# A spectral mixing stage whose blocks run over column wave numbers, with VectorE turning the combined spectrum

## The chip, the cores and the metric

The kernel runs on one NeuronCore of a Trainium2 chip. The metric is the time of one execution on the device, in microseconds (us), lower is better. All data are float32. TensorE (PE) multiplies and transposes into PSUM (8 banks of 512 float32 in each of 128 partitions), VectorE (DVE) and ScalarE (ACT) move PSUM to SBUF, GpSimd (POOL) works on SBUF alone, and SyncE (SP) issues most DMAs.

## The reference, cut to what matters

The program is two blocks of a network on an image of 8 samples, 32 channels, 64 x 64 points: a spectral convolution, a mixture of experts on the tokens, four sweeps of a convolution, and a second mixture of experts. Only the first part, the spectral convolution, is touched:

```
def _L0_conv_ref(x, w1_real, w1_imag, w2_real, w2_imag):     # x: (8, 32, 64, 64), layer-normed over channels
    xf = jnp.fft.rfft2(x, norm='forward')
    w1 = jax.lax.complex(w1_real, w1_imag)                   # each (32 in, 32 out, 32, 32)
    w2 = jax.lax.complex(w2_real, w2_imag)
    top = jnp.einsum('bixy,ioxy->boxy', xf[:, :, :32, :32], w1)
    bot = jnp.einsum('bixy,ioxy->boxy', xf[:, :, -32:, :32], w2)
    out_fft = jnp.zeros((8, 32, 64, 33), dtype=xf.dtype)
    out_fft = out_fft.at[:, :, :32, :32].set(top)
    out_fft = out_fft.at[:, :, -32:, :32].set(bot)
    return jnp.fft.irfft2(out_fft, s=(64, 64), norm='forward')
...
x = x + _L0_conv_ref(_ln_c(x), ...)
```

So each of 64 x 32 kept wave numbers has a complex 32 x 32 matrix of its own, which is applied to 8 samples.

## The kernel before, in words

Everything is written by hand as one instruction list per engine; semaphores are the only order between the lists, and each engine runs its own list strictly in order. The large SBUF regions RA, RB, RCD (halves RC and RD) and RE are reused from step to step. The touched stretch has these steps; "c" is one of 8 chunks of 4 column wave numbers (ky), "g" one of 8 groups of 1024 elements a partition.

- **Turning rows (L511 to L518, `turn_halves` L435).** After the width DFT, TensorE transposes 8 groups of the half spectrum from RC; ScalarE and VectorE drain four each into RA (`t1_pairs`, L802 and L970).
- **Spectrum (L523).** `spectrum(c)`: 8 matmuls with the height DFT table for chunk c into banks 0 to 3 (two chunks in flight). The partitions of the result are 4 samples x 32 channels. `spectrum(0)` waits for all drains, with 20 filler matmuls ahead (`keep_warm`, L483); 30 more stand ahead of the first mix.
- **Spread (`xb_pairs`, L818 on ACT, L990 on DVE).** Each engine copies its half of a chunk into XB (in RB), a matrix that is block diagonal over four groups q of row wave numbers. That takes 16 copies of 32 partitions x 256 elements a chunk, 8 on each engine; consecutive elements are written 512 elements apart.
- **Mix (L539).** 64 matmuls a chunk, against the 2 MB of weights of that chunk, which SP loads from HBM into one of three buffers (L363); the products leave banks 4 to 7 by two ACT copies (L827) and two DVE copies (L999).
- **Turning the products (L560 to L571).** Per chunk TensorE transposes the products with the imaginary and with the real part (16 transposes each); ACT copies the first to `imtmp` (L832); DVE subtracts and adds (L1010, L1011) into V (RA).
- **Turning the spectrum, height DFT back.** TensorE transposes V a second time (`turn_spectrum`, 16 transposes a chunk, ACT drains, L837), and `dft_h(g)` (L584, 8 matmuls a group, two PSUM slots) follows, drained by DVE (`if2_pairs`, L1016).
- **Width DFT back.** `turn_image(g)` (16 transposes, ACT drain L837), `dft_w_back(g)` (L614, 8 matmuls 128 x 128 x 128 with a block-diagonal table), DVE adds the input (L1023) from RC, into which SP reloads the 4 MB of `x_in` (L366) once all products are turned.

ACT's list in the turning stage, which a later step refers to:

```
for c in range(NCH):
    act.wait_ge(s_t1, c + 1)
    if c >= 2:
        act.wait_ge(s_comb, c - 1)
    act.copy(imtmp[:, c % 2, :], banks(4 * (c % 2) + 2, 2)).then_inc(s_tmp, 1)
```

The functions:

Of the kernel before, what the change touches and what calls it, by code (L numbers as in the profile page):

```python
# [9 lines left out]
P = 128  # L10
BL, BH = P // C, B * C // P
TOK = H * W
KY = W // 2
# [28 lines left out]
def build_kernel(nc, x_in, dft, wspec, conv_w, conv_b, gate_w, gate_b, w1, w2, b2, own, out):  # L42
# [5 lines left out]
    with ExitStack() as ctx:  # L48
# [51 lines left out]
        s_tf, s_td = sem("turned_full"), sem("turned_drained")  # L100
# [34 lines left out]
        XB = RB[:, :].rearrange("p (s x z r q b) -> p s x z r q b", s=2, x=X8, z=2 * KYC, r=2, q=Q)  # L135
# [3 lines left out]
        V = RA[:, :].rearrange("p (c x a r n) -> p c x a r n", c=NCH, x=X8, a=2, r=2)  # L139
        V_of_b = RA[:, :].rearrange("p (c m b) -> p c m b", c=NCH, b=B)  # L140
        WR = RE[:, :].rearrange("p (s a x y n) -> p s a x y n", s=3, a=2, x=X8, y=KYC)
        imtmp = RE[:, 0:2 * 1024].rearrange("p (s n) -> p s n", s=2)
# [41 lines left out]

        def turn_slot(g):

            return banks(2 * (g % 2), 2)
# [9 lines left out]
        def t1_pairs(j):  # L197
            g = j - G_T1
            return [(RA[:, 1024 * g:1024 * g + 1024].rearrange("p (n a m) -> p a n m", n=8, a=2),
                     slot(j).rearrange("p (a n m) -> p a n m", n=8, a=2))]  # L200

        def xb_pairs(c, first):
            pairs = []
            for bl in (first, first + 1):
                for q in range(Q):
                    i = PS[C * bl:C * bl + C, 2 * (c % 2):2 * (c % 2) + 2, :].rearrange(
                        "p h (z q r x) -> p q h z r x", q=Q, r=2, x=X8)
                    o = XB[C * q:C * q + C, c % 2, :, :, :, q].rearrange("p x z r (h b) -> p b h z r x", h=BH)
                    pairs.append((o[:, bl], i[:, q]))
            return pairs  # L210
# [4 lines left out]
        def t2_pairs(c):  # L215
            pairs = []
            for bh in range(BH):
                o = RB[:, :].rearrange("p (t k b o) -> p t b k o", t=BH, k=KY, b=BL)[:, bh, :, KYC * c:KYC * c + KYC]
                i = turn_slot(c).rearrange("p (a t b y o) -> p t a b y o", a=2, t=BH, b=BL, y=KYC // 2)[:, bh]
                pairs.append((o.rearrange("p b (a y) o -> p a b y o", a=2), i))  # L220
            return pairs

        def if2_pairs(g):
            o = RD.rearrange("p (t h r k) -> p t r h k", t=BH, h=H, r=2)[:, g % 2, :, :, 8 * (g // 2):8 * (g // 2) + 8]
            return [(o, dft_slot(g).rearrange("p (k r h) -> p r h k", k=8, r=2))]
# [204 lines left out]
        def _(pe):  # L430
# [15 lines left out]

            def centre_group(ln, g):
# [55 lines left out]
            for g in range(8):  # L503
                if g == 3:
                    pe.wait_ge(s_gpc, 1)
                if g >= 4:
                    wait_one_drained(pe, G_T1 + g - 4)
                for n in range(8):
                    m = turn_halves(2 * (g % 4), n, blk(RC, 8 * g + n))
                m.then_inc(s_full, 1)  # L510


            def spectrum(c):
                if c == 0:
                    wait_one_drained(pe, G_T1 + 4)
                    keep_warm(0, 20)
                    wait_drained(pe, G_T1 + 7)
# [3 lines left out]
                for bh in range(BH):  # L521
                    for y in range(KYC):
                        m = pe.matmul(blk(PS[:, 2 * (c % 2) + bh, :], y), blk(RA, bh * KY + c * KYC + y), fwd_h,  # L523
                                      start=True, stop=True)
# [3 lines left out]
            def mix(c):  # L528
                pe.wait_ge(s_xbd, c + 1)
                pe.wait_ge(s_xba, c + 1)  # L530
                pe.wait_ge(s_wc[c % 3], 16 * (c // 3 + 1))
                for k in range(4):
# [12 lines left out]
            for c in range(NCH):  # L545
                if c + 1 < NCH:
                    spectrum(c + 1)
# [674 lines left out]
```

## Time and profile before

| what | value |
|---|---|
| median of 3 runs | 591.72 us (589.74 to 591.88) |
| profiled execution | 587.68 us, its span 585.9 us |
| busy share of the span | PE 90%, DVE 59%, ACT 51%, POOL 20% |
| mean granted TensorE clock | 0.962 |

The profile lists for each engine when an instruction ran, how long the engine was idle before it, and what ended that idle time. A float32 matmul stands there as two passes, so 8 matmuls show as x16; a transpose is one pass. Times inside the span are counted from its start. The touched steps lie between about 42 and 163 us.

### The profile page before, as it was taken

The page shows a single profiled execution, that of the slowest core. Times are in us where ns is not written, and L with a number is a line of the kernel's source. Part 1 is how long each engine was busy: PE and PEld are TensorE (multiplying, and loading weights), DVE is VectorE, ACT ScalarE, POOL GpSimd, SP SyncE. Part 2 cuts the span into 40 slices and gives each one's busy share as a digit, 9 for nine tenths or more (in the row PEclk, how much of TensorE's full clock was granted, in tenths as well). Part 3 has the DMA queues.
Part 4 walks back from the last instruction along what each step waited for, and adds up shares of the span by engine and source line. Part 5 has one row for each costly group of instructions (what it writes and reads, how often), then busy time and mean ns, then how long its engine had stood idle before and what let it go on. Part 6 is the DMA issues. An engine that isn't in the chain of part 4 may idle for free.

```text
span 585.9 us, 25109 instructions
## 1 busy us (share of the span) xinstructions
PE 528.1 (90%) x11076; PEld 472.0 (81%) x11076; DVE 344.6 (59%) x815; ACT 300.3 (51%) x838; POOL 114.7 (20%) x240
## 2 busy tenths in 40 slices
PE   8978997999965999978999999979999999767997
PEld 8978987899964985767888999969998888656873
DVE  2758997734437936773545455435555455569726
ACT  4557997643377502454444444424445777667100
POOL 4000000000034000001333333553331033461000
PEclk9999998999998899998999999979999999978979
DMA  8940882070000000000000023430000244500007
GB/s 347 369 144 2 303 326 96 3 287 1 2 4 2 2 22 0 1 1 2 4 5 3 4 51 74 109 65 6 3 3 4 40 75 80 101 9 1 2 2 288
DMA packets 50260, 41.69 MB, mean 71 GB/s; under 512 B 44998, under 2 KB 45126, under 8 KB 48934
## 3 DMA queue, kind: packets, MB, share of 16 engines
q1 hardware_dynamic: 49304, 38.51, 20.5%
q8 instruction: 89, 1.46, 1.1%
q0 software_dynamic: 704, 1.18, 0.9%
q10 hardware_dynamic: 144, 0.39, 0.2%
q14 instruction: 19, 0.16, 0.1%
HBM read 27.49 MB, written 4.19 MB: 54 GB/s over the span
## 4 chain that ended last, share of the span: by engine, by line
PE 70%; DVE 16%; ACT 5%; POOL 4%; issue 3%; SPq 1%; DMA 0%; POOLq 0%; ACTq 0%; DVEq 0%
PE PS L755 38%; PE PS L724 5%; DVE RB L990 5%; PE PS L483 4%; PE PS L614 3%; PE PS L674 3%; PE PS L584 3%; PE PS L435 2%; PE PS L462 2%; PE PS L539 2%; POOL RE L393 2%; POOL RCD L396 2%; PE PS L492 2%; DVE sums L1032 1%; PE PS L684 1%
## 5 line engine op out<-in xcount | busy, mean ns | idle before, releaser
L755 PE MATMUL PS<-RE,conv_sb 128*64 128x64 f32 x6048 | 231.2, 230 | 4.3 <-DVE RE L1131 3.9
L755 PEld LDWEIGHTS PS<-RE,conv_sb 128*64 128x64 f32 x6048 | 209.1, 139 | 26.4 <-DVE RE L1131 4.6
L880 ACT COPY PS<-convb_sb 128x64 f32<-128x64 f32 x504 | 108.2, 215 | 112.8 <-DVE RE L1143 89.7
L1143 DVE SCALAR_TENSOR_TENSOR RE<-PS,RCD 128x64 f32<-128x64 f32 x252 | 56.7, 225 | 58.0 <-PE PS L755 50.4
L405 POOL COPY RCD<-RE 128x128 f32<-128x128 f32 x126 | 37.4, 297 | 154.3 <-DVE RE L1143 154.2
L1143 DVE SCALAR_TENSOR_TENSOR RE<-PS,RE 128x64 f32<-128x64 f32 x126 | 32.6, 259 | 28.3 <-PE PS L755 26.9
L1143 DVE SCALAR_TENSOR_TENSOR RE<-PS,RB 128x64 f32<-128x64 f32 x126 | 28.4, 225 | 28.1 <-PE PS L755 20.2
L818 ACT COPY RB<-PS 32x256 f32<-32x256 f32 x64 | 40.5, 633 | 7.5 <-PE PS L523 6.7
L990 DVE COPY RB<-PS 32x256 f32<-32x256 f32 x64 | 40.3, 630 | 5.7 <-PE PS L523 4.9
L539 PE MATMUL PS<-RE,RB 128*64 128x64 f32 x1024 | 33.3, 227 | 5.1 <-DVE RCD L999 2.5
L483 PE MATMUL PS<-warm 128*128 128x128 bf16 x468 | 34.3, 239 | 3.9 <-DVE warm L908 1.4
L539 PEld LDWEIGHTS PS<-RE,RB 128*64 128x64 f32 x1024 | 32.2, 142 | 6.5 <-DVE RB L990 3.7
L393 POOL TENSOR_TENSOR RE<-RA 128x1024 f32<-128x1024 f32 x3 | 5.7, 1895 | 160.6 <-ACT RA L851 160.6
L483 PEld LDWEIGHTS PS<-warm 128*128 128x128 bf16 x468 | 31.3, 108 | 4.9 <-ACT RB L858 1.6
L913 DVE TENSOR_REDUCE sums<-RE 128x32 f32<-128x1024 f32 x16 | 19.4, 1218 | 23.2 <-ACT RE L790 23.2
L1032 DVE TENSOR_REDUCE sums<-RE 128x32 f32<-128x1024 f32 x16 | 19.2, 1202 | 19.5 <-POOL RE L393 15.8
L724 PE MATMUL PS<-RCD,espread 128*128 128x512 f32 x64 | 30.5, 632 | 0.0
L837 ACT COPY RB<-PS 128x512 f32<-128x512 f32 (+1 forms) x24 | 16.2, 735 | 25.9 <-PE PS L435 25.9
L790 ACT ACTIVATE RE<-PS 128x1024 f32<-128x1024 f32 x16 | 16.3, 1022 | 23.2 <-PE PS L462 20.1
L405 POOL COPY RB<-RE 128x128 f32<-128x128 f32 x63 | 18.7, 296 | 40.7 <-DVE RE L1143 40.7
L779 ACT COPY RCD<-PS 128x256 f32<-128x256 f32 (+1 forms) x40 | 17.6, 510 | 15.2 <-PE PS L492 7.7
L724 PEld LDWEIGHTS PS<-RCD,espread 128*128 128x128 f32 x64 | 12.8, 206 | 14.9 <-issue 14.4
(116 smaller groups left out, 715.0 us busy)
## 6 DMA issues: line engine op xcount, KB each, us to landing
RE<-wspec SPq DMA_DIRECT2D x8, 2048.0 KB, 8.5
RA<-x_in SPq DMA_DIRECT2D x8, 512.0 KB, 7.4
RCD<-x_in SPq DMA_DIRECT2D x1, 4096.0 KB, 13.7
out<-RA SPq DMA_DIRECT2D x8, 512.0 KB, 2.9
RCD<-RB SPq DMA_DIRECT2D x58, 64.0 KB, 2.6
RE<-RCD SPq DMA_DIRECT2D x32, 80.0 KB, 2.6
conv_sb<-conv_w SPq DMA_DIRECT2D x1, 768.0 KB, 20.0
w_sb<-w SPq DMA_DIRECT2D x2, 264.0 KB
```

Source lines behind the costliest of these rows:

```text
L405: pool.tensor_copy(o, i).then_inc(s_arc, 1)
L483: pe.matmul(PS[:, bank, 0:P], warm[:, :], warm[:, :], start=True, stop=True)
L539: m = pe.matmul(o[:, x % 2, y], XB[:, c % 2, x, 2 * y + a].rearrange("p r q b -> p (r q b)"), WR[:, c % 3, a, x, y, :], start=True, stop=True)
L724: pe.matmul(PS[:, 4 + k % 4, :], espread[:, BL * bh:BL * bh + BL, :].rearrange("p b o -> p (b o)"), rhs, start=True, stop=True).then_inc(s ...
L755: m = pe.matmul(conv_bank(s, u, c)[o:o + OC], conv_sb[:, s, d, o:o + OC], prev, start=False, stop=(d == 2), skip_group_check=True)
L779: m = act.copy(o, i)
L818: m = act.copy(o, i)
L880: act.copy(banks_of, convb_sb[:, s:s + 1].unsqueeze(2).to_broadcast([P, c1 - c0, n])).then_inc(s_seed, 1)
L913: dve.tensor_reduce(sums[:, 32 * g:32 * g + 32], square[:, g % 2, 0:1024].rearrange("p (a c) -> p a c", c=C), AX_X, ALU.add).then_inc(s_su ...
L990: m = dve.tensor_copy(o, i)
L1032: dve.tensor_reduce(sums[:, 32 * g:32 * g + 32], square[:, g % 2, 0:1024].rearrange("p (a c) -> p a c", c=C), AX_X, ALU.add).then_inc(s_su ...
L1143: dve.scalar_tensor_tensor(out=state[:, state_slot(s, u), b0:b1, 1:1 + HO], in0=conv_bank(s, u, c), scalar=0.0, in1=row_at(SRC[s], s, q, u ...
```

## The change

Four things change, all in the stretch above; the rest of the program is as it was, one or more lines lower in the file.

1. The mixing blocks q run over the 4 column wave numbers of a chunk. The rows are turned and drained so that the spectrum of a chunk leaves TensorE with (ky, channel) on its partitions; a chunk is then spread by 4 copies of 32 partitions x 1024 elements in place of 16 of 256. The first two spectra stand between the row groups, and the 50 filler matmuls are gone. The weights are laid out on the host to match.
2. VectorE writes the combined spectrum in another order and turns it itself in 32 x 32 blocks (`dve.transpose`); TensorE's second turn and its ACT drains are gone.
3. The height DFT back, `dft_h(c - 3)`, stands after the products of chunk c in TensorE's list. It has one PSUM slot (banks 6 and 7; group 6 uses banks 0 and 1), and ACT drains it, after `imtmp` of chunk c.
4. The width DFT back is done in four quadrants of 64 x 64, with the nonzero blocks of the table only.

```diff
-        XB = RB[:, :].rearrange("p (s x z r q b) -> p s x z r q b", s=2, x=X8, z=2 * KYC, r=2, q=Q)
+        XB = RB[:, :].rearrange("p (s x r q b) -> p s x r q b", s=2, x=H, r=2, q=KYC)
-        V = RA[:, :].rearrange("p (c x a r n) -> p c x a r n", c=NCH, x=X8, a=2, r=2)
-        V_of_b = RA[:, :].rearrange("p (c m b) -> p c m b", c=NCH, b=B)
+        V = RA[:, :].rearrange("p (c n r x a) -> p c n r x a", c=NCH, n=KYC * B, r=2, x=X8)
+        VT = RB[:, :].rearrange("p (t k n) -> p k t n", t=BH, k=KY)
+        YH = RE[:, WCOLS:WCOLS + NF]
...
+        def product_view(b0):
+            return banks(b0, 2).rearrange("p (a x r n) -> p r n x a", a=2, x=X8, r=2)
+        def dft_h_slot(g):
+            return banks(0 if g == 6 else 6, 2)
...
-        def xb_pairs(c, first):
...
+        def xb_pair(c, q):
+            rows = slice(C * q, C * q + C)
+            i = banks(2 * (c % 2), 2)[rows].rearrange("p (b x r) -> p x r b", b=B, r=2)
+            return XB[rows, c % 2, :, :, q], i
...
         @block.tensor
...
+            def quad(bank, n, lhs, table):
+                for a in range(2):
+                    rows = slice(MO * a, MO * (a + 1))
+                    for o in range(2):
+                        cols = slice(MO * o, MO * (o + 1))
+                        m = pe.matmul(PS[cols, bank + a, MO * n:MO * (n + 1)], lhs[rows, cols], table[rows, rows],
+                                      start=True, stop=True)
+                return m
...
-            spectrum(0)
+            for j in range(8):
+                turn_rows_of(j)
+                if j == 3:
+                    spectrum(0)
+                if j == 5:
+                    spectrum(1)
             for c in range(NCH):
-                if c + 1 < NCH:
+                if 1 <= c < NCH - 1:
                     spectrum(c + 1)
-                if c == 0:
-                    keep_warm(7, 30)
                 mix(c)
...
+            def dft_h(g):
+                pe.wait_ge(s_vt, 2 * (g // 2) + 2)
+                if g == 6:
+                    pe.wait_ge(s_tmp, NCH)
+                elif g >= 1:
+                    pe.wait_ge(s_dr, min(g, 6))
+                for n in range(8):
+                    m = pe.matmul(blk(dft_h_slot(g), n), blk(RB, KY * (g % 2) + 8 * (g // 2) + n), inv_h,
+                                  start=True, stop=True)
+                m.then_inc(s_df, 1)
+            for c in range(NCH):
+                turn_products(c)
+                if c >= 3:
+                    dft_h(c - 3)
+            for g in range(NCH - 3, NCH):
+                dft_h(g)
...
                 for n in range(8):
-                    m = pe.matmul(blk(dft_slot(g), n), blk(RB, 8 * g + n), inv_w, start=True, stop=True)
+                    m = quad(4 + 2 * (g % 2), n, blk(RB, 8 * g + n), inv_w)
...
         @block.scalar
...
-                act.copy(imtmp[:, c % 2, :], banks(4 * (c % 2) + 2, 2)).then_inc(s_tmp, 1)
...
+                act.copy(imtmp[:, c % 2], product_view(0)).then_inc(s_tmp, 1)
+                if c >= 4:
+                    drain_dft_h(c - 4)
+            for g in range(NCH - 4, NCH):
+                drain_dft_h(g)
...
         @block.vector
...
+                by_re, by_im = product_view(2 + 2 * (c % 2)), imtmp[:, c % 2]
+                dve.tensor_tensor(V[:, c, :, 0], by_re[:, 0], by_im[:, 1], ALU.subtract)
+                dve.tensor_tensor(V[:, c, :, 1], by_re[:, 1], by_im[:, 0], ALU.add).then_inc(s_comb, 1)
+                dve.wait_ge(s_comb, c + 1)
+                dve.transpose(VT[:, KYC * c:KYC * c + KYC],
+                              RA[:, 1024 * c:1024 * c + 1024].rearrange("p (k t n) -> p k t n", k=KYC, t=BH)
+                              ).then_inc(s_vt, 1)
```

In the changed `turn_products(c)` TensorE waits for `imtmp` of chunk c - 1 (`s_tmp`), since the imaginary products have one slot (banks 0 and 1), and for the combination of chunk c - 2 (`s_comb`) before the real ones.

**TensorE, from the last mix to the width DFT, before** (L435 transposes, L584 height DFT, L614 width DFT; each row a run of like instructions):

```order
L539 MATMUL PS<-RE,RB 64x2x32 x128
L435 MATMUL PS<-dft_sb,RCD 128x64 x256
L435 MATMUL PS<-dft_sb,RA 128x64 x64
L584 MATMUL PS<-dft_sb,RB 128x128 x16
L435 MATMUL PS<-dft_sb,RA 128x64 x32
L584 MATMUL PS<-dft_sb,RB 128x128 x16
L435 MATMUL PS<-dft_sb,RA 128x64 x32
L584 MATMUL PS<-dft_sb,RB 128x128 x32
L435 MATMUL PS<-dft_sb,RCD 128x64 x32
L614 MATMUL PS<-dft_sb,RB 128x128 x8
```

and now (L436 transposes, L591 height DFT, L454 quadrants of the width DFT):

```order
L550 MATMUL PS<-RE,RB 64x2x32 x128
L436 MATMUL PS<-dft_sb,RCD 128x64 x128
L591 MATMUL PS<-dft_sb,RB 128x128 x8
L436 MATMUL PS<-dft_sb,RCD 128x64 x32
L591 MATMUL PS<-dft_sb,RB 128x128 x8
...
L591 MATMUL PS<-dft_sb,RB 128x128 x32
L436 MATMUL PS<-dft_sb,RE 128x64 x32
L454 MATMUL PS<-dft_sb,RB 64x64 x32
```

The 128 transposes of RA are gone, four chunks of products come first, and single groups of the height DFT stand between the other chunks.

**ScalarE, the same place, now** (L850 `imtmp`, L843 drain of the height DFT, L858 drain of the turned image; before, 8 copies L832 stood together, and the height DFT was drained by VectorE):

```order
L850 COPY RE<-PS 128x1024 x5
L843 COPY RE<-PS 128x2x64x8
L850 COPY RE<-PS 128x1024
L843 COPY RE<-PS 128x2x64x8
L850 COPY RE<-PS 128x1024
L843 COPY RE<-PS 128x2x64x8
L850 COPY RE<-PS 128x1024
L843 COPY RE<-PS 128x2x64x8 x5
L858 COPY RB<-PS 128x2x8x64 x8
```

From the fifth chunk on, each drain of a height DFT group stands behind an `imtmp` copy.

## Rows read from the trace of the kernel before

**Rows 1.** The page's head, and the chain that ended last by engine.

```profile
span 585.9 us, 25109 instructions
...
PE 70%; DVE 16%; ACT 5%; POOL 4%; issue 3%; SPq 1%; DMA 0%; POOLq 0%; ACTq 0%; DVEq 0%
```

**Rows 2.** Windows: four stages, busy us of each engine, granted clock, DMA share, GB/s.

```profile
41.90:55.48 13.58, 11.10 (x212) 10.69 (x211) 10.43 (x15) 9.43 (x13) 0.00 (x0) 1.00 0.01 2
55.48:106.06 50.58, 45.48 (x1121) 43.59 (x1122) 45.27 (x74) 43.21 (x71) 0.00 (x0) 0.97 0.58 211
106.06:139.91 33.85, 32.21 (x515) 30.63 (x513) 18.56 (x23) 16.93 (x25) 0.00 (x0) 1.00 0.31 126
139.91:162.64 22.73, 21.71 (x273) 20.25 (x272) 11.02 (x9) 8.00 (x8) 0.00 (x0) 1.00 0.01 1
```

**Rows 3.** Timeline 39.9 to 56 us: start, us, engine, line, operation, shapes, idle before.

```profile
41.90 4.40 PE L435 MATMUL PS<-dft_sb,RCD 64*128 64x64 f32 x128
...
43.16 4.62 DVE L970 COPY RA<-PS 128x1024 f32<-128x1024 f32 x4 [0.70 <-PE PS L435]
```

**Rows 4.** Timeline 55 to 150 us, one chunk of the mixing stage.

```profile
61.62 3.95 PE L539 MATMUL PS<-RE,RB 128*64 128x64 f32 x128 [0.21 <-DVE RCD L999]
61.99 5.19 DVE L990 COPY RB<-PS 32x256 f32<-32x256 f32 x8
...
65.50 2.05 PE L523 MATMUL PS<-dft_sb,RA 128*128 128x128 f32 x16
...
67.21 1.29 DVE L999 COPY RCD<-PS 128x512 f32<-128x512 f32 x2
```

**Rows 5.** The page's costliest groups: spread on DVE, a VectorE pass over SBUF.

```profile
L990 DVE COPY RB<-PS 32x256 f32<-32x256 f32 x64 | 40.3, 630 | 5.7 <-PE PS L523 4.9
...
L1032 DVE TENSOR_REDUCE sums<-RE 128x32 f32<-128x1024 f32 x16 | 19.2, 1202 | 19.5 <-POOL RE L393 15.8
```

**Rows 6.** Groups by line and form, 106 to 141 us.

```profile
L1016 DVE COPY RCD<-PS 128x1024 f32<-128x1024 f32 x8 | 9.8, 1224 | 13.5 <-PE PS L584 13.5
...
L832 ACT COPY RE<-PS 128x1024 f32<-128x1024 f32 x8 | 8.1, 1015 | 1.7 <-PE PS L435 0.9 <-DVE RA L1011 0.7
...
L1010 DVE TENSOR_TENSOR RA<-PS,RE 128x512 f32<-128x512 f32 x8 | 5.5, 691 | 2.6 <-ACT RE L832 2.6
```

**Rows 7.** Timeline 85 to 107 us, TensorE.

```profile
93.80 1.94 PE L523 MATMUL PS<-dft_sb,RA 128*128 128x128 f32 x13 [2.10 <-issue]
95.67 5.15 PE L539 MATMUL PS<-RE,RB 128*64 128x64 f32 x128
```

**Rows 8.** Windows around two falls of the granted clock.

```profile
96.00:98.00 2.00, 2.00 (x44) 2.00 (x42) 1.96 (x4) 1.97 (x4) 0.00 (x0) 0.50 0.00 0
...
171.00:188.00 17.00, 9.09 (x280) 7.90 (x279) 10.69 (x18) 13.23 (x22) 10.58 (x9) 0.97 0.01 2
188.00:192.00 4.00, 2.72 (x16) 2.33 (x17) 4.00 (x5) 3.31 (x4) 0.00 (x0) 0.50 0.00 0
```

**Rows 9.** The chain in order of time: start, us, what.

```profile
106.13 0.66 PE PS L435 x16
...
121.28 3.77 PE PS L584 x32
...
162.64 1.59 PE PS L648 x64
```

**Rows 10.** Timeline 55 to 150 us, two groups of the width DFT back.

```profile
141.73 2.05 PE L614 MATMUL PS<-dft_sb,RB 128*128 128x128 f32 x16 [0.60 <-ACT RB L837]
...
144.35 2.05 PE L614 MATMUL PS<-dft_sb,RB 128*128 128x128 f32 x16
```

**Rows 11.** SP's issue of the input's reload, and the page's times to landing.

```profile
116.24 0.33 SPq L366 DMA_DIRECT2D RCD<-x_in  x1
...
RE<-wspec SPq DMA_DIRECT2D x8, 2048.0 KB, 8.5
...
RCD<-x_in SPq DMA_DIRECT2D x1, 4096.0 KB, 13.7
```

More of the change, by code:

```diff
@@ L520, in spectrum @@
                     pe.wait_ge(s_xba, c - 1)
[L521 to L524, printed above, removed]
+                for b in range(B):
+                    m = pe.matmul(blk(banks(2 * (c % 2), 2), b), blk(RA, b * NCH + c), fwd_h, start=True, stop=True)
                 m.then_inc(s_f2, 1)
@@ L531, in mix @@
                 pe.wait_ge(s_wc[c % 3], 16 * (c // 3 + 1))
+                if c == 0:
+                    wait_one_drained(pe, 6)
+                    wait_one_drained(pe, 7)
                 for k in range(4):
@@ L806, in _ @@
             norm_tokens(0, f1_pairs)
-            for j in range(G_T1, G_T1 + 8, 2):
-                drain(j, t1_pairs)
             def spread(c):
@@ L816, in spread @@
                     act.wait_ge(s_mix, 4 * (c - 1))
-                for o, i in xb_pairs(c, 2):
+                for q in (2, 3):
+                    o, i = xb_pair(c, q)
                     m = act.copy(o, i)
                 m.then_inc(s_xba, 1)
+            drain(0, t1_pairs)
+            drain(2, t1_pairs)
             spread(0)
+            drain(4, t1_pairs)
+            drain(6, t1_pairs)
             for c in range(NCH):
@@ L827, in _, with drain_dft_h @@
                     act.copy(z_bank(c, k), PS[:, 4 + k, :]).then_inc(s_ma, 1)
+            def drain_dft_h(g):
+                act.wait_ge(s_df, g + 1)
+                for o, i in if2_pairs(g):
+                    m = act.copy(o, i)
+                m.then_inc(s_dr, 1)
             for c in range(NCH):
@@ L831, in _ @@
                     act.wait_ge(s_comb, c - 1)
[L832 to L838 removed]
+                act.copy(imtmp[:, c % 2], product_view(0)).then_inc(s_tmp, 1)
[3 more added lines that the diff above has]
+                drain_dft_h(g)
+            for g in range(8):
+                act.wait_ge(s_tf, g + 1)
+                for o, i in t3_pairs(g):
+                    m = act.copy(o, i)
+                m.then_inc(s_td, 1)
             def experts(l):
@@ L978, in _ @@
             m.then_inc(s_gpc, 1)
-            for j in range(G_T1 + 1, G_T1 + 8, 2):
-                drain(j, t1_pairs)
             def spread(c):
@@ L988, in spread @@
                     dve.wait_ge(s_mix, 4 * (c - 1))
-                for o, i in xb_pairs(c, 0):
+                for q in (0, 1):
+                    o, i = xb_pair(c, q)
                     m = dve.tensor_copy(o, i)
                 m.then_inc(s_xbd, 1)
+            drain(1, t1_pairs)
+            drain(3, t1_pairs)
             spread(0)
+            drain(5, t1_pairs)
+            drain(7, t1_pairs)
             for c in range(NCH):
```

134 lines of the change are left out of this document (43 added, 91 removed).

## The prediction

> **What bounds the kernel now.** I read the page's chain first: TensorE carries 70% of what ended last, VectorE 16% [rows 1]. The change touches only 42 to 163 us, so I cut that into four stages with the windows view [rows 2]: A, rows turned and the first spectra, 13.6 us; B, eight mixes, 50.6 us; C, products to the height DFT, 33.9 us; D, the width DFT, 22.7 us. What follows D waits for its last addition, so what the stages give arrives at the end one for one.
>
> Stage B is the one to look into. The reader is to see that a mix takes TensorE 3.95 us and a spectrum about 1.98 (2.05 with the pipeline's tail), 5.93 together, while VectorE needs 5.19 + 1.29 = 6.48 us for the spread and two drains, and that the mix waits for one of these drains [rows 4]. So VectorE holds the pace by a little, with TensorE right behind. In C TensorE is busy 32.2 of 33.9 us, in D 21.7 of 22.7 [rows 2]: there only less TensorE work, or none waiting, helps.
>
> The sum is made against the profiled execution, 587.68 us; the three runs shown have their median 4.0 us higher, and I carry the difference over to the median.
>
> **A.** Row groups cost 16 transposes of 41 ns, 0.64 us, the 0.66 of [rows 9] less the pipeline's tail; a drain costs 1.02 on ScalarE [rows 6] and 1.19 on VectorE, between the 4.62 / 4 of [rows 3] and the 1.22 of [rows 6]. From the start at 41.9 [rows 3] four groups end at 44.5; VectorE's first drain ends there too; spectrum 0 to 46.6; two more groups and spectrum 1 to 49.8; the last two groups to 51.1. Meanwhile both engines spread chunk 0 from 46.6. A copy of 32 x 1024 is not in the trace. It reads every 128th element of PSUM and writes runs of 8, which is what the drain of the height DFT does on VectorE at 1224 ns for 1024 elements [rows 6]; the old spread, with single elements written 512 apart, takes 630 ns for 256, 2.46 ns each, which would be 2.5 us [rows 5]. I take 1.22 (1.02 on ScalarE), the row of the same pattern, and keep 2.5 as the other end. Then VectorE spreads to 49.0 and drains its two last groups to 52.4, when mix 0 may start, against 55.48: **-3.1 us**. The 50 fillers cost nothing removed: they ran while TensorE waited for those copies.
>
> **B.** VectorE's chunk falls to 2.44 + 1.29 = 3.7 us, below TensorE's 5.93. Eight mixes and six spectra are 8 x 3.95 + 6 x 1.98 = 43.5 us. The weights keep up: each 2 MB is asked for when the mix three chunks back ends, two chunks or 11.9 us ahead of use, and lands in 8.5 us [rows 11]. Late in this stage TensorE stands 2.10 us with nothing shown that it waits for, then is granted half its clock, and a mix takes 5.15 in place of 3.95 [rows 7, 8]. The DMA engines are as full of weights as before, so I expect such a stall again: 2.1 + 1.2 = 3.3 us. 43.5 + 3.3 = 46.8 against 50.6: **-3.8 us** (-7.1 without the stall).
>
> **C.** Removed: TensorE's second turn; what is left of its work, 16 x 0.64 + 8 x 1.88 = 25.3 us, is 7 us under the 32.2 of before. Added: eight VectorE turns of 128 x 1024. No row has one; an ordinary VectorE pass over as many SBUF elements takes 1.20 us [rows 5], the price of 2.46 ns an element would make it 2.5, half a pass 0.6. I take 1.2. VectorE then needs 0.69 + 0.69 + 1.2 [rows 6], some 2.65 us a chunk, 21 us in all, which would fit in less than before. But the lists do not let it be the pace. From chunk 4 on, the single slot makes a ring: 16 imaginary transposes (0.64), `imtmp` on ScalarE (1.02), then behind it in ScalarE's list the drain of the height DFT group of the round before (1.02), and only then may TensorE start the next group (3.77 / 2 = 1.88 [rows 9]), after which come the next imaginary transposes. With 0.13 for two hand-offs a round is 4.7 us, in which TensorE waits about 1.5. Chunks 0 to 3 and the first group take 8.9 us from the end of the mix (`imtmp` 1.7, combined and turned twice to 7.0, group 0 to 8.9); four rounds 18.8; a drain and group 5, 3.0; groups 6 and 7, 3.8. Total 34.5 against 33.9: **+0.6 us**. The turn on VectorE is hidden: its last ends near 27, and group 6 needs it at 30.7; at 2.5 us apiece the start is late and the stage costs 2.5 us more, at 0.6 it costs 0.4 less.
>
> The move has a second price. SP reloads `x_in` when the last product is turned, which now happens 24.3 us into C in place of 10.2. Landing 13.7 us later [rows 11] is at 38.1, and the first addition wants it at 38.3, when the first width DFT (34.5 + two turned images, a drain and 1.60) is done. Before it was there at 129.9 and wanted at 143.8, after the DFT of [rows 10]. 14 us to spare become none: hidden, but any reload later than that shows, softened by two PSUM slots.
>
> **D.** A group before is 2.62 us from DFT to DFT, 1.98 of it matmuls [rows 10]. The quadrant form is one that the kernel has elsewhere: 32 quadrant matmuls with 96 columns, 64 passes, take 1.59 us [rows 9], 24.8 ns a pass. Going by columns 64 would give 1.06, as little gain as none 1.98. I take 1.60, nearest that row. The Trainium skill's TensorEngine Tiling (Array Packing), Instruction Overhead, says that a matmul costs some 60 cycles however few its columns are; the row's 24.8 ns agrees, and the sum by that rule is an estimate of 25 ns x 64 = 1.6. A round is then 1.60 + 0.66 = 2.26, eight of them save 8 x 0.37 = 3.0; the first DFT starts 0.4 later after `turn_image`, as ScalarE first drains the last height DFT group. **-2.5 us** (-6.7 by columns, +0.5 by the full price). ScalarE's 1.02 and VectorE's 1.22 a group stay covered [rows 10].
>
> **Sum:** -3.1 - 3.8 + 0.6 - 2.5 = -8.8 us, 578.9 for the profiled execution and 591.7 - 8.8 = **582.9** for the median.
>
> **The rivals.**
> *1. The spread does not get faster.* If a spread copy keeps 2.46 ns an element, VectorE needs 4.9 + 1.3 a chunk again and A loses 2.8 of its 3.1 us: 6.2 us dearer than forecast, 589.1. For it: nothing in the trace copies 32 partitions faster. Against it: the 2.46 ns stand only where single elements are written far apart [rows 5], and runs of 8 go at 1.2 [rows 6]. Chance 0.07.
>
> *2. Slower: reads that jump through PSUM.* The new spread, `imtmp` and the combination all fetch single elements 64 or more apart, and `product_view` alternates between two banks. If each element so read cost 2.46 ns, the price of the dearest copy here, the spread copies and `imtmp` take 2.5 us and each combination 1.3: rounds of 6.2 us in C, VectorE at 6.3 a chunk in B, 17.3 us dearer, 600.2. It decides from 1.9 ns an element on, where the whole gain is gone. Against it: the height DFT's drain jumps 128 elements at 1.2 ns [rows 6]. The Trainium skill's SBUF — State Buffer, in the box on cachelines under Door 1: The DMA port swizzle, says that PSUM lines hold two float32 and that patterns off them slow matmuls significantly; by that rule this rival is the forecast, and the trace's drain speaks against it for copies. Chance 0.05. With the bank-alternating reads alone at that price it is 10.2 dearer, 593.1; no row has that pattern: 0.06.
>
> *3. The clock falls in C.* TensorE now waits 1.5 us in each round. After its gap of 2.10 us before 93.8 [rows 7] the granted clock was 0.50, 1.2 GHz, and so it was after a stretch in which it worked 9.09 of 17 us [rows 8]. A round at that level costs 0.64 + 1.88 = 2.5 us more; one or two, 585.4 to 587.9. Chance 0.10.
>
> *4. The interleaving is not serial.* If the height DFT groups run beside the products after all, C loses the ring's waits, about 6.1 us: 576.8. That needs ScalarE to drain a group ahead of `imtmp`, which its list doesn't do: 0.04.
>
> The forecast itself has 0.66, with 578 to 586 as its own range: no stall gives 579.6, the quadrants by columns 578.7, at full price 585.9. The remaining 0.02 is for something slower that I don't see.
>
> **How the numbers follow.** About 0.5%, 3 us, is what a measurement can tell from no change. Faster by more: the forecast, rivals 3 and 4, and a small part of the second form of 2, 0.81. Within: rival 1 and most of that form, 0.11. Slower: the rest, 0.08. The range 577.5 to 589.5 holds the forecast but for its edges, rivals 1 and 3, some 0.81.
>
> **What would show it.** Right: spread copies of 32 x 1024 near 1.2 us; mix 0 starting near 52.4; chunks of 5.93 us in which TensorE waits for nothing but a stall; in C rounds of 4.7 us, with L591 waiting for ScalarE's L843; turns near 1.2 us; 64 passes of L454 in 1.6 us; the first addition and the landing of `x_in` within a microsecond of each other. Wrong: copies above 2 us (rivals 1, 2), granted clock 0.5 in C (3), L591 waiting for VectorE's turn, or VectorE's first addition waiting long for the DMA, which would mean that the last product was turned later than worked out.

## The result, and the profile after

The changed kernel takes **575.70 us** (median of 4 runs, 573.13 to 579.15) against 590.73 for the kernel before in the same batch (4 runs): a ratio of 0.9755, interval 0.9716 to 0.9795. That is faster, and below the predicted range; the forecast was 582.9. The profiled execution is the slowest of the four, 579.15 us. All ratios are of executions in the chip's faster state, which leaves out only two of the 12 of one run below.

The page's head and its chain by engine:

```profile
span 577.3 us, 25417 instructions
...
PE 79%; DVE 8%; ACT 6%; POOL 4%; issue 3%; DMA 0%; SPq 0%; POOLq 0%; ACTq 0%; DVEq 0%
```

VectorE's part of the chain has gone from 16% to 8% [rows 1]. Cut at the same four events as [rows 2], the windows are (stretch, its length, busy us of PE, PEld, DVE, ACT and POOL, granted clock, DMA share, GB/s):

```profile
42.40:52.97 10.57, 8.74 (x161) 8.07 (x161) 7.83 (x9) 7.03 (x7) 0.00 (x0) 1.00 0.01 2
52.97:96.78 43.81, 43.60 (x1120) 42.07 (x1121) 27.52 (x32) 21.84 (x29) 0.00 (x0) 1.00 0.67 243
96.78:132.98 36.20, 26.51 (x388) 24.66 (x385) 19.82 (x24) 15.38 (x16) 0.00 (x0) 0.95 0.30 117
...
132.98:151.45 18.47, 15.49 (x657) 14.02 (x656) 9.71 (x8) 8.92 (x9) 0.00 (x0) 1.00 0.02 4
```

| us | A | B | C | D | sum | behind D, to the end |
|---|---|---|---|---|---|---|
| before | 13.58 | 50.58 | 33.85 | 22.68 | 120.69 | 423.3 |
| after | 10.57 | 43.81 | 36.20 | 18.47 | 109.05 | 425.9 |
| forecast change | -3.1 | -3.8 | +0.6 | -2.5 | -8.8 | 0 |
| measured change | -3.0 | -6.8 | +2.35 | -4.2 | -11.6 | +2.6 |

D is cut here at the end of the last addition, 0.05 us ahead of the end in [rows 2]. A is as forecast, B and D gain more, and C loses more. The part behind D was not edited; over 14 profiled executions of this study it took 422.7 to 426.7 us, so single spans are a poor judge here and the stretch is read by itself. It goes with the clock granted there: 0.94 in this trace (425.9 us), 0.95 in the trace of before (423.3) and in a second one of the changed kernel (423.5).

**A and B.** The groups that answer to [rows 5, 6] (spread on DVE and ACT, the turn, one half of the combination, the quadrants):

```profile
L1008 DVE COPY RB<-PS 32x1024 f32<-32x1024 f32 x16 | 19.4, 1214 | 14.7 <-PE PS L532 14.5
...
L826 ACT COPY RB<-PS 32x1024 f32<-32x1024 f32 x16 | 16.1, 1003 | 10.4 <-PE PS L532 10.3
...
L1034 DVE STREAM_TRANSPOSE RB<-RA 128x1024 f32<-128x1024 f32 x8 | 10.0, 1246 | 0.3
L454 PE MATMUL PS<-dft_sb,RB 64*64 64x64 f32 x512 | 9.8, 222 | 2.5 <-issue 1.6 <-ACT RB L858 0.9
...
L1031 DVE TENSOR_TENSOR RA<-PS,RE 128x512 f32<-128x512 f32 x8 | 5.4, 672 | 8.3 <-ACT RE L850 8.3
```

A spread copy takes 1214 ns for 1024 elements where it took 630 for 256, and the turn 1246. TensorE late in B, at the place of [rows 7] ("issue" in the brackets means that the profile shows nothing that the engine waited for):

```profile
86.69 2.05 PE L532 MATMUL PS<-dft_sb,RA 128*128 128x128 f32 x16
88.67 1.15 PE L550 MATMUL PS<-RE,RB 128*64 128x64 f32 x32
89.98 6.87 PE L550 MATMUL PS<-RE,RB 128*64 128x64 f32 x224 [0.16 <-issue]
```

The stop of 2.10 us with nothing to wait for has shrunk to 0.16 and stands elsewhere: 32 passes into mix 6, where it stood 3 passes into spectrum 7. No half clock (a granted clock of 0.50, the 1.2 GHz level) follows: the last 224 passes of the mixes run at 31 ns each.

**C.** A round, on TensorE and then on ScalarE:

```profile
118.10 2.02 PE L591 MATMUL PS<-dft_sb,RB 128*128 128x128 f32 x16 [1.61 <-ACT RE L843]
120.06 1.22 PE L436 MATMUL PS<-dft_sb,RCD 64*128 64x64 f32 x32
122.89 3.37 PE L591 MATMUL PS<-dft_sb,RB 128*128 128x128 f32 x16 [1.61 <-ACT RE L843]
```

```profile
120.81 1.01 ACT L850 COPY RE<-PS 128x1024 f32<-128x1024 f32 x1 [2.86 <-PE PS L436]
121.72 1.02 ACT L843 COPY RE<-PS 128x1024 f32<-128x1024 f32 x1
```

The height DFT waits 1.61 us for the drain of the group before (L843), which stands behind `imtmp` (L850): the ring of the prediction, 4.78 us a round. The fourth round's DFT takes 3.37 us in place of 2.02, and the window over it shows why:

```profile
124.00:126.00 2.00, 2.00 (x11) 1.96 (x10) 0.50 (x1) 0.00 (x0) 0.00 (x0) 0.50 1.22 524
```

**D.** Quadrant groups (L454) and the transposes between them, against [rows 10]:

```profile
135.07 1.16 PE L454 MATMUL PS<-dft_sb,RB 64*64 64x64 f32 x64 [0.87 <-ACT RB L858]
136.16 0.71 PE L436 MATMUL PS<-dft_sb,RE 64*128 64x64 f32 x16
136.80 1.16 PE L454 MATMUL PS<-dft_sb,RB 64*64 64x64 f32 x64
...
142.14 1.03 PE L454 MATMUL PS<-dft_sb,RB 64*64 64x64 f32 x52
143.98 0.45 PE L454 MATMUL PS<-dft_sb,RB 64*64 64x64 f32 x12 [0.81 <-issue]
...
146.74 0.56 PE L454 MATMUL PS<-dft_sb,RB 64*64 64x64 f32 x19
148.13 1.85 PE L454 MATMUL PS<-dft_sb,RB 64*64 64x64 f32 x109 [0.83 <-issue]
```

64 passes take 1.09 us from start to the next instruction's start, and the period is 1.73 where it was 2.62. Two stops without a cause in the profile are new.

### The profile page after: what moved, and what is told of

Read it like the earlier page. It is cut to its first block, busy times and chain, and to the rows that moved or that the text cites. A ratio compares the mean times of both kernels' runs of the same rounds, so it can differ in the third digit from the quotient of the medians.

```text
span 577.3 us, 25417 instructions
## 1 busy us (share of the span) xinstructions
PE 516.2 (89%) x11282; PEld 462.0 (80%) x11282; DVE 323.8 (56%) x767; ACT 275.8 (48%) x782; POOL 113.3 (20%) x240
## 4 chain that ended last, share of the span: by engine, by line
PE 79%; DVE 8%; ACT 6%; POOL 4%; issue 3%; DMA 0%; SPq 0%; POOLq 0%; ACTq 0%; DVEq 0%
PE PS L766 40%; PE PS L550 6%; PE PS L494 5%; PE PS L735 5%; PE PS L591 3%; PE PS L532 3%; PE PS L685 3%; PE PS L473 2%; POOL RE L394 2%; PE PS L436 2%; POOL RCD L397 2%; PE PS L503 2%; DVE sums L1052 1%; PE PS L454 1%; PE PS L468 1%
## 5 line engine op out<-in xcount | busy, mean ns | idle before, releaser
L494 PE MATMUL PS<-warm 128*128 128x128 bf16 x418 | 35.6, 261 | 3.9 <-DVE warm L929 1.4
L494 PEld LDWEIGHTS PS<-warm 128*128 128x128 bf16 x418 | 32.6, 120 | 5.1 <-ACT RB L879 1.6
L550 PEld LDWEIGHTS PS<-RE,RB 128*64 128x64 f32 x1024 | 30.9, 138 | 2.8 <-issue 2.0
L1008 DVE COPY RB<-PS 32x1024 f32<-32x1024 f32 x16 | 19.4, 1214 | 14.7 <-PE PS L532 14.5
L591 PE MATMUL PS<-dft_sb,RB 128*128 128x128 f32 x128 | 17.1, 294 | 7.9 <-ACT RE L843 7.6
L591 PEld LDWEIGHTS PS<-dft_sb,RB 128*128 128x128 f32 x128 | 16.0, 205 | 8.7 <-issue 8.3
## 6 DMA issues: line engine op xcount, KB each, us to landing
RCD<-x_in SPq DMA_DIRECT2D x1, 4096.0 KB, 12.3
```

What stands on the lines that cost most here:

```text
L494: pe.matmul(PS[:, bank, 0:P], warm[:, :], warm[:, :], start=True, stop=True)
L550: m = pe.matmul(o[:, x % 2, y], XB[:, c % 2, 2 * KYC * x + 2 * y + a].rearrange("p r q b -> p (r q b)"), WR[:, c % 3, a, x, y, :], start=T ...
L591: m = pe.matmul(blk(dft_h_slot(g), n), blk(RB, KY * (g % 2) + 8 * (g // 2) + n), inv_h, start=True, stop=True)
L1008: m = dve.tensor_copy(o, i)
```

## The experiments

Each kernel was timed beside the kernel before on the same chip. Two repeats say what such a comparison is worth.

**Repeats.** The changed kernel again, and the kernel before again, without an edit.

> The changed kernel once more, for a second trace. Theory 1 (the gain beyond the forecast is made inside the changed stretch: the quadrant matmuls cost about 1.0 us a group, and the stall in the mixing stage did not come): the stretch from the first row group to the last addition takes 107 to 110 us again, as in the first trace of it (109.1) against 120.7 before, and the ratio to the kernel before stays at 0.972 to 0.980. Theory 2 (part of the gain is luck of the executions, in the unchanged rest behind the stretch): the stretch is the same, but the rest, 425.8 us in the first trace, differs by several us between the two traces, with the granted clock.

577.21 us, ratio 0.9775 (0.9749 to 0.98). In its trace A 10.57, B 43.19, C 36.41, D 18.47, sum 108.64; again one round of the height DFT at half clock (3.54 us, another round than in the first trace), and a stop of 0.16 us, 32 passes into mix 6.

> The kernel before once more, for a second trace. Theory A (the stall of 2.1 us and the half clock behind it in the mixing stage belong to that program under that load of weight transfers): they are there again at the same instruction of spectrum 7, and the stage takes 50.6 us. Theory B (they come by chance): the stage takes about 47 us in this trace. The ratio to the kernel before is 1.00 either way; its spread shows how far single executions differ.

589.30 us, ratio 0.9969 (0.9946 to 0.9993) to its own twin: 0.3% is the ground on which the other ratios stand. Its stretch takes 121.40 us. Against this run the repeat of the changed kernel gains 12.1 us by the medians and 12.8 by the stretch. The stop stands again 3 passes into spectrum 7, and B takes 51.21 us:

```profile
93.77 1.61 PE L523 MATMUL PS<-dft_sb,RA 128*128 128x128 f32 x13 [1.83 <-issue]
```

No half clock follows it here; that comes one mix later, behind a wait of 2.52 us for VectorE.

### Where the stall of the mixing stage went

**Fillers out of the kernel before.**

```diff
-                    keep_warm(0, 20)
...
-                if c == 0:
-                    keep_warm(7, 30)
```

> The kernel before without its 20 + 30 filler matmuls. In all three traces with them TensorE stops for about 2 us three passes into spectrum 7, with nothing shown that it waits for, while the last weights arrive; in the three traces of the changed kernel it stops for 0.16 us, 32 passes into mix 6, when the weights are in. Theory 1 (the stop is tied to the count of instructions in TensorE's list, and the fillers decide which matmul it meets): without them it moves some 50 passes later, into mix 6, and shrinks; the mixing stage takes 47.5 to 49.5 us in place of 50.6 to 51.7, ratio 0.995 or lower, unless the clock, no longer held up by the fillers, takes some back. Theory 2 (the stop belongs to the place, the wait of spectrum 7): it stays at spectrum 7 with about 2 us.

590.09 us, ratio 0.9967 (0.9935 to 1.0). TensorE's first mix and its last two, and then, from the kernel before, VectorE's spread of the last chunk:

```profile
55.65 6.42 PE L538 MATMUL PS<-RE,RB 128*64 128x64 f32 x128 [3.64 <-DVE RB L987]
...
95.52 3.95 PE L538 MATMUL PS<-RE,RB 128*64 128x64 f32 x128 [0.19 <-DVE RCD L996]
101.63 5.50 PE L538 MATMUL PS<-RE,RB 128*64 128x64 f32 x128 [2.15 <-DVE RCD L996]
```

```profile
95.78 5.53 DVE L990 COPY RB<-PS 32x256 f32<-32x256 f32 x8 [2.72 <-PE PS L523]
```

No stop without a cause is left, and yet B takes 51.41 us, as before (50.58 and 51.21). That does not make the stall of [rows 7] free in the kernel before. VectorE sets the pace there, and it stood 2.72 us behind the stall: from mix 5 to mix 6 it is 9.20 us before (86.47 to 95.67) and 6.12 here (89.40 to 95.52). What the missing stall gives, 3.1 us, the clock takes back. Without the fillers TensorE stands 3.64 us ahead of mix 0 and runs it at half clock, 6.42 us for 3.95; the next mix starts 8.33 us after it, where before that took 6.14. The last mix, behind a wait of 2.15 us, takes 5.50, as in the repeat of before, and 3.95 in its first trace. So theory 1 was right that the stop leaves spectrum 7, and its time failed by the exception that it made, the clock.

**Fillers back into the changed kernel**, 50 short matmuls ahead of the first mix, behind the same waits.

```diff
+            pe.wait_ge(s_xbd, 1)
+            pe.wait_ge(s_xba, 1)
+            for _ in range(50):
+                pe.matmul(PS[0:32, 0, 0:8], warm[:, 0:32], warm[:, 0:8], start=True, stop=True)
```

> The changed kernel with 50 small filler matmuls (32 x 8, one pass each) ahead of the first mix. They take some 1.5 us where TensorE waits 1.4 us for VectorE's last drain, so the first mix starts at most 1 us later. Theory 1 (count of instructions): the stop moves from mix 6 back to the start of spectrum 7, about 1.2 us earlier against the weights, and grows to 1 to 2.5 us: the mixing stage takes 44.5 to 46 us in place of 43.2 to 43.8. Theory 2 (place): stop stays where it is, at 0.2 us, stage 43.2 to 43.8 us.

581.72 us, ratio 0.9855 (0.9818 to 0.9892), 0.8% above the repeat. A does not move (10.59), but B is 48.59. TensorE, and two windows over the stop and behind it:

```profile
83.80 3.50 PE L550 MATMUL PS<-RE,RB 128*64 128x64 f32 x114
89.78 3.65 PE L532 MATMUL PS<-dft_sb,RA 128*128 128x128 f32 x16 [2.48 <-issue]
```

```profile
88.00:89.00 1.00, 0.00 (x0) 0.00 (x0) 0.00 (x0) 0.00 (x0) 0.00 (x0) 1.00 0.00 0
...
90.00:92.00 2.00, 2.00 (x10) 2.00 (x11) 0.00 (x0) 0.00 (x0) 0.00 (x0) 0.50 0.03 8
```

The stop is back with 2.48 us, the half clock behind it costs 1.6 (3.65 for 2.05), and a smaller stop of 0.70 stands 128 passes of mix ahead of it: 4.8 us together, the whole growth of B over the first trace (43.81). It moved from 32 passes into mix 6 to the start of spectrum 7, which is 48 passes earlier for 50 added ones. And it ends at nearly the same moment, 89.78 us here and 89.98 in the changed kernel, 9.1 and 9.0 us behind the issue of the last weights: what TensorE needs arrives then, and 50 instructions decide how long it has stood there by that time.

**Fewer bytes of weights**, with the fillers in.

```diff
-                sp.dma_start(RE[:, WCOLS * (c % 3):WCOLS * (c % 3 + 1)], wspec[c]).then_inc(s_wc[c % 3], 16)
+                w = WCOLS if c < 3 else WCOLS // 8
+                sp.dma_start(RE[:, WCOLS * (c % 3):WCOLS * (c % 3) + w], wspec[c][:, :w]).then_inc(s_wc[c % 3], 16)
```

> The changed kernel with the 50 short matmuls of the earlier run ahead of the first mix, and with the last five of the eight loads of weights cut to an eighth of their columns (the rest of each buffer keeps the weights of an earlier chunk, so the values of chunks 3 to 7 are other ones). Theory: TensorE stops late in the mixing stage because the block of its instructions that it has come to lands only after the weights, whose transfers fill the DMA engines until then; with an eighth of the bytes no stop over 0.3 us is left there, no half clock behind it, and B is 43.2 to 43.8 us, as in the changed kernel, where the full weights and the same 50 matmuls gave 48.6. The time is 575 to 577.5. Rival: the stop belongs to the place in the instruction list and not to the transfers; then TensorE stops again some 2.5 us at the start of spectrum 7, B is 48.6 and the time near 582.

575.14 us, ratio 0.9737 (0.9687 to 0.9786); B is 42.79. The same place:

```profile
85.87 2.05 PE L533 MATMUL PS<-dft_sb,RA 128*128 128x128 f32 x16
87.85 7.68 PE L551 MATMUL PS<-RE,RB 128*64 128x64 f32 x256
```

No stop and no half clock, with the instruction list of the run before. From 81 to 87 us the share of the DMA engines is 0.15 here and 0.93 there. So the stop takes two things: a place in the list, and DMA engines filled by the weights. What is fetched there is read off the page's DMA queues (packets, MB, share) of the changed kernel and, in the second fence, of a later run with 512 more passes, each of which comes with a weight load:

```profile
q8 instruction: 90, 1.47, 1.2%
```

```profile
q8 instruction: 94, 1.54, 1.1%
```

1024 more instructions are 4 more packets in the queue named "instruction", 256 to a packet of some 16 KB; the run with the full table, which has 768 fewer, shows 3 fewer (87). The packets also come when TensorE needs them: in the run with the 50 matmuls and full weights this queue moves nothing between 82.2 and 87.1 us and one packet between 87.1 and 88.1, and the stop ends at 89.78.

The Trainium skill, Runtime: NRT & Kernel Launch, Instruction fetch mechanics, says that an engine's instructions are streamed in 16 KiB blocks of 256 by a DMA queue of its own, and that this is mostly hidden. The packets here agree with the size; the stops of 0.16 to 2.48 us do not agree with the second half.

### What a quadrant costs

**The changed kernel with the full table.**

```diff
-                    m = quad(4 + 2 * (g % 2), n, blk(RB, 8 * g + n), inv_w)
+                    m = pe.matmul(blk(dft_slot(g), n), blk(RB, 8 * g + n), inv_w, start=True, stop=True)
...
```

> The changed kernel with the width DFT back by full 128 x 128 matmuls, as before the change. Theory 1 (a quadrant group costs about 1.03 us against 1.98): a group takes 2.62 us again in place of 1.73, eight of them 7.1 us more, less the two stalls of 0.8 us if they do not come: 5.5 to 7 us slower than the changed kernel, ratio to before 0.983 to 0.988. Theory 2 (the quadrants are worth what was forecast, 3.0 us, and the extra gain lies elsewhere): 3 us slower, ratio near 0.980.

580.84 us, ratio 0.9819 (0.9785 to 0.9852). D is 22.94, 4.5 us above the quadrants', with no stop in it: the groups are those of theory 1, but the stops that go with the quadrants cost more than its 1.6 us, and by the medians the loss against the repeat is 3.6 us, between the two theories. C again has one DFT at half clock (3.63).

**The kernel before with quadrants**, the same edit turned round.

> The kernel before with the quadrant width DFT alone. Theory 1 (by columns): the last stage goes from 22.7 to about 15.6 us (period 1.73), 7 us faster, ratio 0.988. Theory 2 (by the overhead of each matmul): period 2.26, 3 us faster, ratio 0.995.

587.87 us, ratio 0.9955 (0.9929 to 0.998). D is 18.67, 4.0 us less than in the repeat of before, with three stops of 1.8 us in all. So the groups are again those of theory 1 (64 passes in 1.09 us), while the time is the one that theory 2 gave: by the medians only 1.4 us arrives against the repeat of before. In the profiled execution the part behind D took 426.7 us against 422.7, at a granted clock of 0.94 against 0.95. Whether the earlier start moves a fall of the clock there wasn't tried.

**Each quadrant matmul in two halves of 32 columns.**

```diff
-                        m = pe.matmul(PS[cols, bank + a, MO * n:MO * (n + 1)], lhs[rows, cols], table[rows, rows],
-                                      start=True, stop=True)
+                        for h in range(2):
+                            w0 = MO // 2 * h
+                            m = pe.matmul(PS[cols, bank + a, MO * n + w0:MO * n + w0 + MO // 2], lhs[rows, cols],
+                                          table[rows, MO * a + w0:MO * a + w0 + MO // 2], start=True, stop=True)
```

> The changed kernel with each 64-column quadrant matmul of the width DFT split into two of 32 columns, 128 passes a group where there were 64, the same products. Theory: quadrant passes are paid by their columns, about 16 ns for 64; then a group stays near 1.1 us, and only twice as many TensorE instructions are read in, so that stops of 0.8 us with nothing shown to wait for grow from two to four or more (D 18.5 plus 1 to 3 us). Rival: a pass has a price of its own of about 16 ns or more however few its columns; then a group takes 2.1 us, D about 26.5 (8 us more), the time about 584.

590.06 us, ratio 1.0027 (0.9998 to 1.0057); D is 33.30. TensorE in the first groups:

```profile
133.81 2.13 PE L456 MATMUL PS<-dft_sb,RB 64*64 64x32 f32 x128 [0.86 <-ACT RB L860]
135.86 0.71 PE L436 MATMUL PS<-dft_sb,RE 64*128 64x64 f32 x16
...
138.78 0.68 PE L456 MATMUL PS<-dft_sb,RB 64*64 64x32 f32 x26 [0.46 <-issue]
139.40 0.71 PE L436 MATMUL PS<-dft_sb,RE 64*128 64x64 f32 x16
140.04 1.58 PE L456 MATMUL PS<-dft_sb,RB 64*64 64x32 f32 x86
142.59 0.91 PE L456 MATMUL PS<-dft_sb,RB 64*64 64x32 f32 x42 [0.97 <-issue]
```

Half the columns cost the same: 128 passes in 2.05 us are 16 ns each, like 64 columns (1.09 / 64 = 17). So the rival was right on the pass and the theory on the stops, and both are paid. From stop to stop there are 26 + 16 + 86 = 128 passes, and 127 or 128 each time to the end, that is 256 instructions with the weight loads: one packet. Seven stops stand between 138.78 and 161.73, one every 3.8 us: that is how fast packets come here. Without the DFT's half clock in this trace C is 34.84 us, which prices that fall at 1.4 in the changed kernel.

### The ring of the height DFT

**ScalarE drains the height DFT ahead of `imtmp`.**

```diff
+                if c >= 4:
+                    drain_dft_h(c - 4)
                 act.copy(imtmp[:, c % 2], product_view(0)).then_inc(s_tmp, 1)
-                if c >= 4:
-                    drain_dft_h(c - 4)
```

> The changed kernel with ScalarE's drain of a height DFT group ahead of the imtmp copy of the same round, in place of behind it. Theory 1 (the ring of im transposes, imtmp, drain, height DFT sets the pace of stage C): TensorE no longer waits 1.6 us in each round, the fall of the clock in the ring goes too, and stage C takes about 28.5 us in place of 36.3; the reload of the input, issued when the last product is turned, then lands later than the first addition wants it, which gives back about 1 us. Net 5 to 7 us faster than the changed kernel, ratio 0.966 to 0.970. Theory 2 (VectorE's combination and turn set the pace): stage C changes by under 1 us.

573.59 us, ratio 0.9711 (0.9674 to 0.9749). C falls to 28.59:

```profile
106.44 2.02 PE L591 MATMUL PS<-dft_sb,RB 128*128 128x128 f32 x16
108.39 1.22 PE L436 MATMUL PS<-dft_sb,RCD 64*128 64x64 f32 x32
109.65 2.02 PE L591 MATMUL PS<-dft_sb,RB 128*128 128x128 f32 x16
```

Rounds are 3.21 us with no wait and no fall of the clock. Against the repeat the stretch is 5.4 us shorter, within the 5 to 7 expected, and the median 3.6. D grows to 20.10. SP's reload, issued at 116.08, now is what the first addition waits for, and TensorE's stops have grown:

```profile
128.40 1.22 DVE L1042 TENSOR_TENSOR RCD<-PS,RCD 128x1024 f32<-128x1024 f32 x1 [8.87 <-DMA RCD<-x_in]
```

```profile
137.19 0.45 PE L454 MATMUL PS<-dft_sb,RB 64*64 64x64 f32 x12 [1.09 <-issue]
...
141.61 1.85 PE L454 MATMUL PS<-dft_sb,RB 64*64 64x64 f32 x109 [1.11 <-issue]
```

The wait itself costs little: the addition starts 3.57 us into D, where it starts at 3.38 with the reload early (the next run), and TensorE waits for no addition. The stops are 2.84 us in four, where the changed kernel has 1.64 in two.

**And the reload earlier.** It writes only the half of RCD that the first four chunks use, so it need not wait for the other four.

```diff
-            sp.wait_ge(s_t0, NCH)
-            sp.wait_ge(s_t1, NCH)
+            sp.wait_ge(s_t0, NCH // 2)
+            sp.wait_ge(s_t1, NCH // 2)
```

> The same with the reload of the input issued when the fourth product is turned (its region holds the first four chunks only). Theory 1: the first addition no longer waits for the DMA, 1 us less than with the drain alone, stage D back to 18.5 us. Theory 2 (the reload was never late): no difference to the drain alone.

**568.04 us** (565.79 to 572.1), ratio 0.9629 (0.9592 to 0.9667): the best version, faster than both kernels. The reload is issued at 102.91, the first addition waits for TensorE alone, TensorE's stops are 1.79 us in two, and D is 18.48 again; the stretch is 101.22 us. So in these two traces the late reload costs D 1.6 us, by TensorE's stops and not by the addition. D's first packet of instructions comes some 2.5 us into the stage with the reload late and 1.1 with it early, which fits 4 MB in the way until 128.4; a run that shows it was not made. The medians of the two runs differ by 5.6 us, of which 2.0 lie in the stretch; the rest is open.

**The turn twice.**

```diff
+                dve.transpose(RE[:, 2048:3072], RA[:, 1024 * c:1024 * c + 1024])
```

> The changed kernel with a second turn of the same size in each chunk on VectorE, whose output nothing reads. Theory: the turn is hidden behind TensorE's ring from chunk 4 on, so that only the start and the last groups feel it: VectorE then needs 0.69 + 0.69 + 2.5 = 3.9 us a chunk against rounds of 4.8, C is 36.3 plus 1.3 to 2.5 us, the time 577 to 579. Rival: VectorE's turn sets the pace of C; then C is longer by 8 x 1.25 = 10 us, the time about 586.

580.80 us, ratio 0.9865 (0.9819 to 0.991). C is 40.12, 3.9 us more than after: two DFT groups ran at half clock in place of one (3.35 and 3.49 us), some 1.5 of it, and the late start is the other 2.4. The time is above the 577 to 579 of the theory by about that second fall. The turns do not set the pace: the rounds between stay at 4.78.

### What made the spread cheap

**Writes 32 elements apart**, the same bytes and the same shape of copy.

```diff
-            i = banks(2 * (c % 2), 2)[rows].rearrange("p (b x r) -> p x r b", b=B, r=2)
-            return XB[rows, c % 2, :, :, q], i
+            i = banks(2 * (c % 2), 2)[rows].rearrange("p (b x r) -> p b x r", b=B, r=2)
+            return XB[rows, c % 2, :, :, q].rearrange("p x r b -> p b x r"), i
```

> The changed kernel, but each spread copy runs through its 1024 elements in the order (sample, x, part): PSUM is read along runs, and consecutive elements are written 32 elements apart, the same bytes to the same places. Theory: what made the old spread cost 2.46 ns an element is the distance between consecutive writes; then a copy takes about 2.5 us on VectorE, two of them and two drains 6.3 us a chunk, VectorE sets the pace of the mixing stage again, and A and B together lose about 3 to 6 us (time 580 to 583). Rival: the copies got cheaper only because one has 1024 elements and not 256 (a fixed price per copy); then a copy stays at 1.2 us and the time at that of the changed kernel, 575 to 577.

582.50 us, ratio 0.9887 (0.9836 to 0.9938). The spread on DVE, and one stop of TensorE, 104 passes into mix 2:

```profile
L1008 DVE COPY RB<-PS 32x1024 f32<-32x1024 f32 x16 | 31.0, 1940 | 11.1 <-PE PS L532 11.0
```

```profile
72.39 0.92 PE L550 MATMUL PS<-RE,RB 128*64 128x64 f32 x24 [2.26 <-issue]
```

1.89 ns an element lie between the two theories: at equal shape, reading in jumps and writing in runs is 1.6 times cheaper than reading in runs and writing in jumps. A grows to 12.25. But VectorE does not set B's pace (2 x 1.94 + 2 x 0.69 = 5.3 us, under 5.93); B grows to 49.61, of which the stop, with the half clock that follows (3.28 us for a spectrum), is 3.5, mix 0 at half clock 1.3 (5.26 us), and a wait of the last mix for VectorE 0.7. The stop is again at a border of a packet, 504 passes ahead of that in the changed kernel, four packets but for the few other instructions.

## Why the prediction was wrong

**A was right**, by its parts: the copy was taken at 1.22 and 1.02 us and takes 1.21 and 1.00; mix 0 starts 10.57 us after the first turn for a forecast of 10.5. Rivals 1 and 2 fall with it: spread 1.2 ns an element, `imtmp` 1.01 us, the bank-alternating combination 0.67 for 0.69 before.

The Trainium skill, SBUF — State Buffer, the box on cachelines under Door 1: The DMA port swizzle, was weighed there as a rule on jumping reads of PSUM; no copy here shows it.

**B failed, by the largest error of the sum.** "The DMA engines are as full of weights as before, so I expect such a stall again: 2.1 + 1.2 = 3.3 us." The sum of mixes and spectra, 43.5, was right (43.19 and 43.81 measured); the stall came to 0.16. It is not a matter of full DMA engines alone: a packet of 256 instructions must be due while they are full. Taking out 50 fillers moved that border 45 passes on, to where the packet had all but landed. "The 50 fillers cost nothing removed" was wrong for the same reason: 50 short matmuls put back cost 4.8 us, 32 to 39 us later. In the kernel before the fillers had two sides that the prediction did not see: they held the clock for mix 0, worth 2.5 us of TensorE there, and they put the border where the stop was long. The stop was a real part of the 50.58, 3.1 us by mix 5 to mix 6; its return is what was wrongly taken for granted.

**C: the mechanism was right and one term was missing.** The ring runs as worked out: 4.78 us a round for 4.7, 8.9 us to the end of the first group for 8.9, the turn 1.25 for 1.2. Without a fall of the clock C is 34.84 for a forecast of 34.5. What was missing is rival 3, given 0.10: after waits of 1.6 us one DFT group ran at the 1.2 GHz level, in six of seven traces of this code, for 1.4 to 1.6 us (only the group, so less than the 2.5 a round that the rival asked). In the two kernels without these waits it did not occur. Why it takes one round and not another stays open. The reload and the first addition, thought to meet, are 2.8 us apart: it lands 12.3 us after 121.31, at 133.6, and the addition starts at 136.37, behind TensorE.

**D: one term mis-sized.** "I take 1.60, nearest that row." It is 1.09, the end "by columns". The row of 24.8 ns a pass had 96 columns and could be read two ways; 128 columns in 124 ns [rows 10], as if four quadrants ran side by side, are 23 ns for 96 and 15.5 for 64, and I took a price per pass. Six periods shorter by 0.89 and the last two groups, with no transposes between them, shorter by 1.5 are 6.8 us; the two stops take 2.1 back (142.14 to 144.36 is 2.22 us for a group of 1.09, 146.74 to 149.91 is 3.17 for two), and 0.5 goes at the start, the end and one slower group: 4.2.

The Trainium skill, TensorEngine Tiling (Array Packing), Instruction Overhead, gave the 60 cycles that agreed with 24.8 ns. Passes of 64 and of 32 columns at 16 to 17 ns contradict it here, where four quadrants take turns, and the measurement decides: there is a floor for a pass, but at two thirds of that.

**The whole.** B (-3.0 against forecast), D (-1.7) and C (+1.75) leave 11.6 us gained in the stretch where 8.8 were forecast. That alone would put the median at 580, inside the range given. By medians the gain is 15.0 in the first batch and 13.7 and 12.1 with the repeats; the repeat of before alone shifts by 0.3%, and what the medians gain beyond the stretch, up to 3.4 us, is not explained by anything shown. Without it the time would have stayed in the range, so the steps above are the errors of the sum, and not all of the miss. The range was too narrow for a reason of its own: it took each other price by itself (no stall 579.6, quadrants by columns 578.7). Both came, and together they make 575.4; that this is near the 575.7 measured is luck, as the stops in D and the fall of the clock in C took some 4 us of it back. The rival of an interleaving that is not serial did not happen, but its price, 6.1 us, was near what the exchange of two lines in ScalarE's list brought (C 34.84 to 28.59).

## What to carry to other kernels

Count instructions as a resource: TensorE's list arrives in packets of 256, and where passes are as short as 16 ns, or the DMA engines are full, a packet can come late; adding or removing a few dozen cheap instructions far ahead moves such a stop, so a stall "with nothing shown that it waits for" should be priced only after asking where the border falls. Before taking fillers out, look at what they hold: the clock of the next matmuls, and the place of such a border. A range that takes each rival alone is too narrow when two of them can come together. A row that two rules explain (24.8 ns: by columns or by pass) is no evidence between them. On an engine with a strict order, put the copy that frees the single slot ahead of the one that has a spare buffer.

## What the runs showed of the hardware

- TensorE's instructions come by a DMA queue in packets of 256 (512 more passes with their weight loads: 4 more packets; 384 fewer: 3 fewer). In the run with halved quadrants one packet came every 3.8 us, 15 ns an instruction, with the DMA engines at a share of 0.02. A mix of 128 passes needs 3.95 us a packet, so it runs just below that rate.
- A quadrant pass costs 16 ns with 32 columns and 17 with 64.
- A 32 x 32 block turn of 128 x 1024 float32 on VectorE takes 1.25 us, like a plain pass over as many elements [rows 5].
- A copy from PSUM of 32 x 1024 takes 1.21 us with jumping reads and writes in runs of 8, and 1.94 with the jumps on the writing side.
- After TensorE has stood 1.6 to 2.5 us, its granted clock was 0.50 in most traces, at a price of 1.2 to 1.6 us, but not behind each of several equal waits (four of 1.61 us: behind one of them in six traces, behind none in one).
